# A mixing product in split fp32r parts in place of one fp32 product, in a Perceiver block with experts

## What is computed

```
x = x + xattn(layernorm(x), ctx, Wq, Wk, Wv, Wo)      # first layer
m = layernorm(x)                                      # y in the kernel, per batch 32 x 1024
logits = einsum('bcl,bdl->bcd', m, m)                 # 32 x 32 per batch
probs = softmax(max(logits, -1) - logits)
read = einsum('bcd,bdl->bcl', probs, m)               # the weighted sum of rows
x = x + eta * read + m                                # second layer
x = x + experts(layernorm(x), top 2 of 8)             # third layer
```

## Time and profile before

| | us |
|---|---|
| median of 3 runs | 1273.03 |
| lowest, highest run | 1269.46, 1277.02 |
| span of the profiled execution | 1263.3 |
| TensorE busy in it | 1126.6 (89%) |
| vector engine busy | 679.6 (54%) |
| scalar engine busy | 441.1 (35%) |
| mixing, first projection product to the last plan row | 773.5 to 968.0 |

### The profile page before, as it was taken

How to read it: one execution, slowest core, us unless ns; L and a number is a source line. 1 busy time by engine, 2 the same in 40 slices (tenths; PEclk the granted TensorE clock), 3 DMA queues, 4 the chain that set the end, 5 groups by cost and what they waited for, 6 DMA issues and landing times. The chain is left out here.

```text
span 1263.3 us, 27032 instructions
## 1 busy us (share of the span) xinstructions
PE 1126.6 (89%) x8474; PEld 994.7 (79%) x8475; DVE 679.6 (54%) x1699; ACT 441.1 (35%) x1111; POOL 259.9 (21%) x436
## 2 busy tenths in 40 slices
PE   6997989999999999999999987999942989989795
PEld 5886889899999999999999965777732867867684
DVE  5442146566666666666666655566675344354441
ACT  3232134444444444444444443111223033323120
POOL 0000211111211111111111101123232323333432
PEclk9999799999999999999999986999965989989898
DMA  7225355465565565565565461543151665566421
GB/s 283 67 109 200 105 169 155 151 198 149 155 198 153 164 184 154 163 184 164 156 182 172 130 218 52 203 84 67 70 164 50 231 222 177 195 212 229 155 97 65
DMA packets 72737, 196.95 MB, mean 156 GB/s; under 512 B 14800, under 2 KB 17232, under 8 KB 68592
## 3 DMA queue, kind: packets, MB, share of 16 engines
q1 hardware_dynamic: 52368, 145.66, 37.1%
q0 software_dynamic: 18016, 42.29, 11.0%
q10 hardware_dynamic: 2304, 8.39, 1.7%
HBM read 159.07 MB, written 44.56 MB: 161 GB/s over the span
## 5 line engine op out<-in xcount | busy, mean ns | idle before, releaser
L593 ACT ACTIVATE prob<-bank,nmax 128x257 f32<-128x257 f32 x256 | 122.2, 478 | 327.1 <-DVE nmax L648 326.8
L648 DVE TENSOR_REDUCE nmax<-bank 128x1 f32<-128x257 f32 x256 | 107.7, 421 | 170.4 <-PE bank L783 170.0
L690 PE MATMUL bank<-cT_h,wkv_h 128*128 128x256 f32 x512 | 157.3, 307 | 0.0
L699 PE MATMUL bank<-wkv_h,cT_h 128*128 128x256 f32 x512 | 154.5, 302 | 0.0
L1441 PE MATMUL bank<-w_h,gT_h 128*128 x320 | 131.4, 411 | 23.6 <-DVE gT_l L1387 23.6
L690 PE MATMUL bank<-cT_h,wkv_l 128*128 128x256 f32 x512 | 145.0, 283 | 0.0
L690 PE MATMUL bank<-cT_l,wkv_h 128*128 128x256 f32 x512 | 144.8, 283 | 0.0
L699 PE MATMUL bank<-wkv_h,cT_l 128*128 128x256 f32 x512 | 144.0, 281 | 0.0
L699 PE MATMUL bank<-wkv_l,cT_h 128*128 128x256 f32 x512 | 144.0, 281 | 0.0
L1441 PE MATMUL bank<-w_h,gT_l 128*128 x320 | 128.5, 401 | 0.0
L1441 PE MATMUL bank<-w_l,gT_h 128*128 x320 | 128.3, 401 | 0.0
(11 more groups left out here) (199 smaller groups left out, 2273.1 us busy)
## 6 DMA issues: line engine op xcount, KB each, us to landing
kcat<-k_scratch SPq DMA_DIRECT2D x128, 258.0 KB, 4.2
cx<-in_context SPq DMA_DIRECT2D x32, 1024.0 KB, 5.4
raw<-in_expert_w SPq DMA_DIRECT2D x48, 512.0 KB, 4.1
qcat<-q_scratch POOLq DMA_DIRECT2D x128, 128.0 KB, 5.1
k_scratch<-kT_h SPq DMA_DIRECT2D x32, 258.0 KB, 2.3
k_scratch<-kT_l SPq DMA_DIRECT2D x32, 258.0 KB, 2.5
x_in<-in_x SPq DMA_DIRECT2D x16, 512.0 KB, 4.2
expert_raw<-in_expert_w SPq DMA_DIRECT2D x16, 512.0 KB, 8.1
```

Source lines behind the costliest of these rows:

```text
L593: act.activation(prob[:, 1 - par, s, 0:SK], s_ps[s % 2][:, 0:SK], ACT.Exp, bias=nmax[:, 1 - par, s:s + 1], accum_out=sums[:, 1 - par, s:s ...
L648: dve.reduce_max(nmax[:, 1 - par, s:s + 1], s_ps[s % 2][:, 0:SK], AXX, negate=True).then_inc(max_done, 1)
L690: o = pe.matmul(k_ps[:, j * 256:(j + 1) * 256], wkv[x][:, k, j * P:(j + 1) * P], cT[y][:, par, k, :], start=(j == 0 and k == 0 and n == 0) ...
L699: o = pe.matmul(v_ps[:, a * KV:(a + 1) * KV], cT[x][:, par, k, a * P:(a + 1) * P], wkv[y][:, k, KV:2 * KV], start=(a == 0 and k == 0 and n ...
```

## The change

The two fp32 products of the weighted sum become six fp32r products, by the same three passes as the projection. For that both operands are split. y is split into `y_h` by the scalar engine (behind the copies of yT) and `y_l` by the vector engine. The turned weights `probT` are split into `probT_h` (scalar engine, behind the exponentials) and `probT_l` (vector engine). Both subtractions stand at the end of the vector engine's step, between the transposes and the scale. TensorE waits for `y_l_ready`, which the last subtraction raises, where it waited for `probT_ready`. To make room in SBUF the table `no_tokens` moves into a shared region and `start` is folded into `reached`.

```diff
@@ tiles and semaphores
+        probT_s = [sb("probT_h", [P, P], F32R), sb("probT_l", [P, P], F32R)]
+        y_s = [sb("y_h", [P, D], F32R), sb("y_l", [P, D], F32R)]
-        no_tokens = sb("no_tokens", [P, 2 * ROWS // P], I32)
+        no_tokens = sh.at("no_tokens", STAGE + 12 * D, [P, 2 * ROWS // P], I32)
-        start = sb("start", [1, COLS, E], F32)
@@ scalar engine, tile t-1 in step t
                     copy_turned(yT, turned_before(t))
+                    if not known(t) or t >= 2:
+                        act.wait_ge(r_done, 2 * (t - 1))
+                    act.wait_ge(y_ready, t)
+                    act.activation(y_s[0][:, :], y[:, 1 - par, :], ACT.Copy).then_inc(y_h_ready, 1)
...
                                    accum_out=psum_row[:, :]).then_inc(prob_ready, 1)
+                    act.wait_ge(probT_ready, t)
+                    act.activation(probT_s[0][:, :], probT[:, :], ACT.Copy).then_inc(probT_h_ready, 1)
@@ vector engine, end of step t
                     o.then_inc(probT_ready, 1)
+                    dve.wait_ge(y_h_ready, t)
+                    dve.tensor_tensor(y_s[1][:, :], y[:, 1 - par, :], y_s[0][:, :].bitcast(F32), ALU.subtract)
+                    dve.wait_ge(probT_h_ready, t)
+                    dve.tensor_tensor(probT_s[1][:, :], probT[:, :], probT_s[0][:, :].bitcast(F32), ALU.subtract).then_inc(y_l_ready, 1)
                     dve.wait_ge(psr_ready, t)
@@ vector engine, plan
-            then(dve.tensor_tensor(start[:, :, :], reached[:, :, :], first_b, ALU.mult))
             then(dve.tensor_reduce(e_f[:, 0, :], reached[:, :, :], AXX, ALU.add))
-            then(dve.tensor_reduce(e_f[:, 1, :], start[:, :, :], AXX, ALU.max))
+            then(dve.tensor_tensor(reached[:, :, :], reached[:, :, :], first_b, ALU.mult))
+            then(dve.tensor_reduce(e_f[:, 1, :], reached[:, :, :], AXX, ALU.max))
@@ TensorE, ahead of unit 2
-                        pe.wait_ge(probT_ready, t - 1)
+                        pe.wait_ge(y_l_ready, t - 1)
                         for h in range(2):
                             if not known(t) or t >= 3:
                                 pe.wait_ge(z_ready, 2 * (t - 3) + h + 1)
-                            pe.matmul(r_ps[h][:, :], probT[:, :], y[:, par, h * 512:(h + 1) * 512], start=True, stop=True).then_inc(r_done, 1)
+                            for m, (a, b) in enumerate(PASSES):
+                                o = pe.matmul(r_ps[h][:, :], probT_s[a][:, :], y_s[b][:, h * 512:(h + 1) * 512], start=(m == 0), stop=(m == 2))
+                            o.then_inc(r_done, 1)
```

More of the change, by code:

```diff
@@ L898, in mixing @@
             sem("t_done"), sem("t_copied"), sem("g_done"), sem("low_ready"), sem("prob_ready"), sem("probT_ready"))
+        y_h_ready, y_l_ready, probT_h_ready = sem("y_h_ready"), sem("y_l_ready"), sem("probT_h_ready")
         psr_ready, scale_ready, r_done, z_ready, x3_ready, n_ready = (
```

## The result

| | before | after |
|---|---|---|
| median | 1271.24 us (4 runs) | 1284.37 us (4 runs) |
| lowest, highest | 1267.33, 1277.02 | 1283.73, 1285.40 |
| span of the profiled execution | 1263.3 | 1282.1 |
| TensorE busy in it | 1126.6 | 1135.3 |
| vector engine busy | 679.6 | 689.6 |

The changed kernel takes 1.0098 of the time of the one before (95% interval 1.0073 to 1.0124): it is slower, and the forecast of 1280.5 us had the sign right and the size too small. Its ratio on the 1273.03 us that the forecast started from gives +12.5 us (1285.5) instead of +7.5. That lies inside the range of 1273.5 to 1287.0. Between the two profiled executions 4.7 us arose ahead of mixing, in code that the edit leaves alone. From the last plan row to the end of the span both take the same (295.5 and 295.6 us). So mixing accounts for all that can belong to the edit: +14.0 us in this pair of executions.

The account below looks back on a forecast made before the run. The prediction took a ring through the vector engine in mixing as the bound. Terms +0.55, +6.75, -0.17, -0.1 and -0.7 gave +6.3 us, one more clock fall +1.2: 1273.0 + 7.5 = 1280.5 us, range 1273.5 to 1287.0.

Parts of the forecast that it names:

- The ring of the earlier trace: In mixing, vector engine and TensorE wait for each other; vector work between n and x2 costs its length each turn.
- TensorE's own saving: In the weighted sum, split products save 0.35 us per step, 2.8 us only if TensorE set the pace everywhere.
- The cost of the operations: At the step end, y_l costs 1.13 us and probT_l 0.22; probT_h, under 0.6 us, lies beside y_l.
- the lateness of x2: The two subtractions ahead of the scale delay the next tile's x2 by 1.35 us per step end.
- The early step ends and the last steps: Ends of steps 1 and 2 together add 0.55 us; end of step 8 adds nothing; step 9 saves 0.7.
- The term of 1.35 for each end of step: Ends of steps 3 to 7 each pay the subtractions' full 1.35 us, 6.75 us together.
- The wait for n: TensorE's wait for n in the loop, 1.25 us before, was to rise by 0.35 us.
- The clock term: TensorE's longer stretch of gate products and waiting lowers its granted clock in one more loop turn, adding 1.2 us.
- the 0.17 above: In step 6, where the result waited for TensorE after a clock fall, its first half is ready 0.17 us sooner.
- the rival with all four falls: TensorE's clock falls in all four loop turns: +9.9 us, 1282.9 us; no separate chance given.
- the collision with GpSimd: GpSimd's slot stores hold the subtractions at the step end, up to 1 us more at five ends: 1285 us, chance 0.08.
- dearer subtractions: Upper bound at the step end: 1.6 us instead of 1.35 if neither subtraction overlaps its neighbours, sum up to 9 us.

Follow-up runs that it names:

- e1: The changed kernel without the subtractions y_l and probT_l, its six products using high parts only; ratio 1.0012 to the kernel before, 1276.06 us against 1274.23.
- e3: The changed kernel with y_l moved behind ot_l and probT_l into the next tile's wait for rstd; ratio 1.0006 to the kernel before.
- e7: The changed kernel with a second operation of y_l's size at the step end and twelve unused products behind the gate; ratio 1.0122 to the kernel before.
- e8: The changed kernel with only y_l moved behind ot_l, probT_l left at the step end; ratio 1.0046 to the kernel before.
- e4: The changed kernel with seven unused products of 512 columns behind the gate in each loop step; ratio 1.0057 to the kernel before.
- e5: e3 with three unused products of 512 columns per loop step, one amid the gate products and two behind; ratio 1.0018 to the kernel before.
- e9: e3 with four of the eight gate products put ahead of the last three products of unit 7; ratio 1.0054 to the kernel before.
- e2: The changed kernel with its splitting operations kept and the fp32 product put back; ratio 1.0100 to the kernel before.
- e6: The kernel before with three unused products of 512 columns per loop step, one amid the gate products and two behind; ratio 1.0002 to the kernel before.
- e10: The kernel before with four of the eight gate products put ahead of the last three products of unit 7; ratio 1.0050 to the kernel before.

## Why the prediction came out as it did

**What bounds the kernel: right.** The ring of the earlier trace rows closes through the vector engine. e1 (work away, loss away), e3 (work moved, loss away) and e7 (1.13 us more, turn 1.1 longer at the same clock) each show it, and e1 agrees with the other half: TensorE's own saving is worth nothing that can be measured.

**The cost of the operations: right.** y_l took 1.22 to 1.27 us in the loop, probT_l 0.28, and the lateness of x2 was 1.33 for 1.35. probT_h took 0.31 us beside y_l and was never waited for; in e8, where its cover is gone, it was. The wait for x2 rose to 1.80, 2.15, 1.85 and 2.02 us, for 1.8 forecast.

**The early step ends and the last steps: about right.** Terms of +0.55 and -0.7. Measured are +0.75 ahead of the turn that shrank to 18.00 us and -0.64 in that turn, so +0.1 together, and for the last distance -0.52. At the end of step 9 the result waited 2.05 and 0.43 us instead of 3.55 and 0.86.

**The term of 1.35 for each end of step: too large by 0.45 in the first three turns, from something not seen.** The wait for n did not rise by 0.35; it fell from 1.25 to between 0.95 and 1.00. From the start of the result to the start of n are 7.02 us and were 7.47. The vector engine of the changed kernel behind the result, one turn before the one above:

```profile
849.94 1.44 DVE L1086 SCALAR_TENSOR_TENSOR n<-bank,scale,y 128x512 f32<-128x512 f32 x2 [2.28 <-PE bank L1238]
...
851.92 0.16 DVE L1126 TENSOR_TENSOR gap<-top 128x1 f32<-128x1 f32 x1
...
852.38 0.96 DVE L1128 CAST chosen_f<-top_i 128x2 f32<-128x2 uint32 x1
```

GpSimd's addition beside it:

```profile
850.77 2.54 POOL L989 TENSOR_TENSOR x<-x,n 128x512 f32<-128x512 f32 x2 [3.96 <-DVE n L1086]
```

In the earlier trace rows it was `gap` that GpSimd's addition held for 1.25 us, with the two index operations queued behind it. Now the result takes 1.44 us instead of 1.55 to 1.61, and `gap` starts 1.98 us behind the start of the result instead of 2.09 to 2.23. GpSimd's second half starts, by an estimate from the rows, about 2.1 us behind it (850.77 plus half of 2.54, less 849.94), so `gap` slips in ahead and is free at 0.16 us, and the CAST is held for 0.96 instead, with less waste around it. Over the other kernels this goes with the product, with one exception: in the first three of the four turns `gap` took 0.16 to 0.19 us in the changed kernel, e3, e4, e5, e7, e8 and e9 (split products), and 1.12 to 1.30 us in the kernel before, e2, e6 and e10 (fp32 product). e1 has both: in two turns `gap` started 1.94 us behind the result and took 0.19, in the other it started 2.09 behind and took 1.29. So the start decides there, and not the kind of product. No run moved `gap` alone, so the start order as the cause is argued from the rows and not shown.

**The clock term: the mechanism right, the size wrong, and this is the step that failed.** The text said "I take one more" fall, and "one costs 21.47 - 20.10 = 1.37 us, less the 0.17 above: 1.2". Measured are four falls, and e4 puts them at 8.9 us together, 2.2 each. Both halves were too small, for turns that did not lose alike: twelve slow products (2.4 us) in three of them and about six in the fourth come to nearly the same sum. The number: the text itself had the stretch grow from 2.4 to 3.7 us, and the rival with all four falls was there (+9.9), yet only one more was taken. The price was read from one fall that reached seven products behind the wait (1.4 us), while one that comes earlier in the stretch covers all twelve up to the weighted sum (2.4 us). Four falls at 1.2 would have given +9.9; at 2.2, less the gain at `gap`, the sum comes out near the measured one. What makes the clock fall in one turn and not in another stays open, so the number of falls could be bounded but not worked out.

**The range: held, in part by luck.** The text gave 1282.9 us for falls in all four turns, and 1285.5 was measured. The room above 1282.9 was there for the collision with GpSimd (1285) and for dearer subtractions, and neither came; the dearer falls filled it.

| term, us | forecast | measured |
|---|---|---|
| lateness of x2 in the four turns | 5.4 | 5.3 (4 x 1.33) |
| gain at `gap` in them | 0 | about -1.4 (3 x 0.45; the fourth had none to gain, its `gap` took 0.32 before) |
| the one fall of before, gone | -1.37 | -1.37 |
| falls after | +2.3 (two at 1.2, less 0.1 in step 7) | +8.9 (four) |
| idle time ahead of `low` in the second and fourth turn | 0 | +0.5 (0.35 + 0.12) |
| sum over the four turns | 6.3 | 11.9 |

The four turns grew by 11.8. Without the falls before and after, the measured terms come to 4.4 us, and e4 left 4.3 for the ring. The row on `low` is a term that the forecast lacked. The vector engine idles ahead of the minimum of the logits, first before, then after, both in the second turn:

```profile
853.89 0.19 DVE L1094 TENSOR_REDUCE low<-bank 128x1 f32<-128x32 f32 x1 [0.24 <-DVE slot L1135]
...
863.56 0.19 DVE L1102 TENSOR_REDUCE low<-bank 128x1 f32<-128x32 f32 x1 [0.59 <-DVE slot L1147]
```

This idle time is 0.24 us in every turn of before, e1, e6 and e10. In every kernel with the two subtractions in the vector engine's loop, e3 with its moved ones among them, it is longer in the second turn (0.59, in e7 0.49) and in the fourth (0.36 or 0.37, in e7 0.27). No run shows what it is. The fifth end of step brought 1.38.

**Collision with GpSimd: right that it does not hold the vector engine, wrong in a sentence about the stores.** y_l was never slowed beyond 1.27 us. But the text said that the rule of shared ports does not agree with the slot stores. The other way round it can, as the changed kernel shows once in the loop, where the vector engine started first (841.41):

```profile
841.41 1.22 DVE L1112 TENSOR_TENSOR y_l<-y,y_h 128x1024 fp32r<-128x1024 f32 x1
```

GpSimd's stores in the changed kernel, there and in the next two turns:

```profile
841.49 1.98 POOL L996 DMA_INDIRECT slot_scratch<-entries,slot  x1 [0.30 <-issue]
...
864.81 0.96 POOL L996 DMA_INDIRECT slot_scratch<-entries,slot  x1 [0.30 <-issue]
...
888.58 0.96 POOL L996 DMA_INDIRECT slot_scratch<-entries,slot  x1 [0.30 <-issue]
```

The store took 1.98 us instead of 0.96, and so it did at this place in e2, e4 and e7. Nobody waits for it there. In the third turn y_l started first again, but only 0.01 us ahead (888.57), and the store took its usual 0.96, y_l 1.27 instead of 1.23; all other such pairs, 0.01 to 0.02 us apart, read the same. The Trainium skill, "SBUF — State Buffer", section "SBUF: two separate sides", says that of a vector operation with two SBUF inputs and a GpSimd operation that reads SBUF, whichever starts first has the port pair for its whole instruction. The store from 841.49 agrees. The one from 888.58, 0.01 us behind y_l, does not, and a store which started first did not hold y_l either (from 864.81, beside y_l from 865.14, which ran its usual 1.23 us).

**The profiled execution.** I carried +7.5 over unscaled. An execution's own time lies 1.6 us above its span (1283.76 and 1282.1), so before's profiled one took some 1264.9 us, by this estimate, where its lowest timed run took 1266.22. Most of the 9.7 us between span and median was the spread of its executions. The difference of two profiled executions (1282.1 - 1263.3 = 18.8) therefore overstates the change.

## What to carry to other kernels

Where two engines wait for each other around a ring, work on one of them costs about its full length even if the other is busy 90% of the time; look for the wait in the ring that can take it (here the wait for rstd and the place behind ot_l) before pricing the edit. A longer wait of TensorE can have a second price, here larger than the wait itself: where the granted clock falls in it, the products up to the next point where someone waits for TensorE run at half speed. Count the products between the two, not the mean over a turn, and where the clock already falls in some turns give the case that it falls in all of them a price and a good chance.

## What the runs showed of the hardware

- Seven extra products of 512 columns per turn (1.8 us) behind the gate went with a clock of 1.00 in all four turns of the profiled execution and took their sum from 92.70 to 83.82 us (ratios 1.0098 and 1.0057); twelve of them with a longer step end did not (0.93, 0.93, 1.00, 0.92).
- Splitting a run of 8-column products around three large ones cost 0.5% in two kernels, with falls in 8 of 8 turns of their two profiled executions.
- A CAST of two columns with a single input in SBUF was held by GpSimd's two-input addition (0.96 us against 0.17), so it is not only operations with two inputs that are held.
- A two-input subtraction of 128x1024 that started 0.08 us ahead went with an indirect store of GpSimd of 1.98 us instead of 0.96, in four kernels. With 0.01 to 0.02 us between them the store took 0.96 and the subtraction 1.27 instead of 1.23; with the store 0.10 us or more ahead neither was held.
